# Moving the clamp of the up half from VectorE to GpSimd in a fused adaLN block

## The chip, the cores and the metric

One Trainium2 chip, one core of it. The metric is device microseconds (us) of the whole kernel, lower is better. Engine names are those of the profile: PE (TensorE), with its weight loads as PEld, DVE (VectorE), ACT (ScalarE), POOL (GpSimd), SP (SyncE, which here only issues DMAs).

## The reference, cut to what matters

The input is 8 sequences of 512 tokens of width 128, all in float32. The block is a linear-recurrent "attention" layer followed by a mixture of 8 experts, each behind a modulated layernorm. The change touches the experts alone:

```python
x = x + ga * attn(layernorm(x) * (1 + ca) + sa)     # a scan over the 512 tokens
h = layernorm(x) * (1 + cb) + sb
gate_up = einsum('nd,ejd->nej', h, gate_up_proj) + gate_up_proj_bias   # E = 8, I = 256
gate, up = split(gate_up, 2, axis=-1)
gate = minimum(gate, 7.0)
up = clip(up, -7.0, 7.0)
act = (up + 1.0) * gate * sigmoid(1.702 * gate)
out = einsum('nei,edi->ned', act, down_proj) + down_proj_bias
y = einsum('ned,ne->nd', out, combine)              # softmax over the top 4 of 8 experts
```

## The kernel before

**Tiling and stages.** The tokens are worked through in 16 chunks of 256 (two tiles of 128 rows, 8 sequences x 16 steps each). A chunk passes through seven stages, one iteration of the outer loop apiece: `a` (first layernorm, residual), `g` (gate logits), `e` (softmax of the gates), `s` (the scan of 32 steps), `p` (output projection, second layernorm, router), `m` (the experts) and `o` (write out). In one iteration each engine works on up to seven chunks, each in another stage, so there are 22 iterations. Stage `s` runs in iterations 3 to 18, stage `m` in 5 to 20; iterations 6 to 15 hold all seven stages.

**Order of work.** Every engine has its own instruction stream, written out by hand, and executes it strictly in order; semaphores (`Event`, with `at(c, n)` for the n-th increment of chunk c) tie the streams together. On DVE the scan sets the order: for each step t it issues the products `L758`, then the sums `L766`, and between them the function `between(u, ...)` puts in the other work by slot number u = 3t, 3t+1, 3t+2, thus 96 slots an iteration. Expert k of the stage `m` owns nine slots from u = 22 + 9k on: `clamp_up` (`L831`) at r = 0, and the two halves of `hidden` (`L844`) at r = 3 and 4. Other slots used below: the row sums `L741` at u = 9 to 26 with the reciprocals `L749` at 18 and 28, the row maxima `L734` at odd u from 33 to 67, the output gate `go` (`L896`) at 47 and 49, the statistics of the second layernorm (`L901`) at 56 and 57, and its normalisation `xh2` (`L728`) at 68 and 69.

**One expert.** PE multiplies `h2t` with the up and gate weights (`L997`, in the function `gate_up`, which waits until the activation of expert k-2 is done); ACT evicts the up half to SBUF and adds bias + 1 (`L598`), then puts Silu over the gate half in PSUM (`L604`); `clamp_up` limits the up half in place to 1-7 .. 1+7; `hidden` multiplies both into `act_t`; PE multiplies with the down weights (`L1010`); ACT weighs the result (`L615`); POOL adds it to `yacc` (`L460`, `accumulate`). `up` and `act_t` have two buffers each, by k % 2. `hidden(m, k, 0)` waits for the Silu, for `clamp_ok` and for the down matmul that frees its `act_t` buffer.

**PE's order** within iteration: gate_up(0), gate_up(1), the transposes of the router weights, down(0), bias matmul `L1043`, gate_up(2), the transposes of `yt_tok`, down(1), gate_up(3), the output projection `wo` (`L1031`, on which `go` waits), down(2), gate_up(4), down(3), gate_up(5), down(4), and so on, with the gate logits `L984` in between.

**POOL's order** in an iteration: inverse square root and first h of stage `a`, `finish` of stage `o`, `gate_value(e,0)`, two `norm_gates` (`L407`), `gate_value(e,1)`, accumulate 0, `norm_gates`, `norm_gates`, accumulate 1, `residual`, `sub_max` (`L414`), `new_residual` (`L445`), accumulate 2, `sub_max`, `inv_sqrt` (`L390`, `L393`), accumulate 3, `sub_max`, `second_h` (`L450`, `L452`, it waits for `xh2`), `inv_sqrt`, accumulate 4, `sub_max`, accumulate 5 and 6.

Of the kernel before, what the change touches and what calls it, by code (L numbers as in the profile page):

```python
# [18 lines left out]
ALU = mybir.AluOpType  # L19
# [6 lines left out]
LIMIT = 7.0  # L26
# [21 lines left out]
def adaln_block(nc, x, norm_w, w_v, w_a, w_out, router_w, router_b, gu_w, gu_b, down_w, down_b, cond, w_mod, out):  # L48
# [27 lines left out]
    with ExitStack() as ctx:  # L76
# [87 lines left out]
        up = sb("up", [P, 2, KI * N])  # L164
# [206 lines left out]
        def _(pool):  # L371
# [24 lines left out]
            def gate_value(e, j):  # L396
                pool.wait_ge(zs_ok.sem, zs_ok.at(e, H * (j + 1)))
                v = ex[:, j, :].rearrange("p (r k) -> p r k", k=M1)
                nc.gpsimd.tensor_tensor(v[:, :, 0], v[:, :, 0], vv[:, j, :], ALU.mult).then_inc(rv_ok.sem, 1)

            def norm_gates(e, j, part):
                if part == 0:
                    pool.wait_ge(rz_ok.sem, rz_ok.at(e, j + 1))
                    pool.wait_ge(rv_ok.sem, rv_ok.at(e, j + 1))
                lo, hi = part * HI // 2, (part + 1) * HI // 2
                v = ex[:, j, :].rearrange("p (r k) -> p r k", k=M1)[:, lo:hi, :]
                nc.gpsimd.tensor_tensor(v, v, rz[:, j, lo:hi].unsqueeze(2).broadcast_to([P, HI // 2, M1]),  # L407
                                        ALU.mult).then_inc(norm_ok.sem, 1)
# [19 lines left out]
            def residual(a):  # L428

                if not is_first(a):  # L430
                    for j in range(TILES):
                        pool.wait_ge(res_st[j].sem, res_st[j].at(a, 0))
                pool.wait_ge(h_ok.sem, h_ok.at(a, 1))
                nc.gpsimd.tensor_tensor(res[:, :, :], hh[:, :, :], both(2), ALU.mult).then_inc(gh_ok.sem, 1)
                pool.wait_ge(gh_ok.sem, gh_ok.at(a, 1))
                nc.gpsimd.tensor_tensor(res[:, :, :], res[:, :, :], xg[:, :, :], ALU.add).then_inc(res_ok.sem, 1)
# [17 lines left out]
            def accumulate(m, k):  # L454
# [3 lines left out]
                else:  # L458
                    pool.wait_ge(acc_ok.sem, acc_ok.at(m, k))
                nc.gpsimd.tensor_tensor(yacc[:, :, :], yacc[:, :, :], weighted[:, k % 2, :, :], ALU.add  # L460
                                        ).then_inc(acc_ok.sem, 1)

            def finish(o):
                accumulate(o, E - 1)
                pool.wait_ge(acc_ok.sem, acc_ok.at(o, E))
                nc.gpsimd.tensor_tensor(gy[:, :, :], yacc[:, :, :], both(5), ALU.mult).then_inc(gy_ok.sem, 1)
                if not is_first(o):
                    for j in range(TILES):
                        pool.wait_ge(out_st[j].sem, out_st[j].at(o, 0))
                pool.wait_ge(xm_ld.sem, xm_ld.at(o, 16))  # L470
                pool.wait_ge(gy_ok.sem, gy_ok.at(o, 1))
                nc.gpsimd.tensor_tensor(res_out[:, :, :], gy[:, :, :], xm[:, :, :], ALU.add).then_inc(ro_ok.sem, 1)

            def run(a, g, e, s, p, m, o):
                if a is not None:
                    pool.wait_ge(mv1_ok.sem, mv1_ok.at(a, TILES))
                    inv_sqrt(mv1[:, :, 1], eps_mean, ve1, rs1, ve1_ok, rs1_ok, a)
                    first_h(a)
                if o is not None:
                    finish(o)  # L480
                if e is not None:
                    gate_value(e, 0)
                    norm_gates(e, 0, 0)
                    norm_gates(e, 0, 1)
                    gate_value(e, 1)
                if m is not None:
                    accumulate(m, 0)
                if e is not None:
                    norm_gates(e, 1, 0)
                    norm_gates(e, 1, 1)  # L490
                if m is not None:
                    accumulate(m, 1)
                if a is not None:
                    residual(a)
                if g is not None:
                    sub_max(g, 0, 0)
                if p is not None:
                    new_residual(p)
                if m is not None:
                    accumulate(m, 2)  # L500
                if g is not None:
                    sub_max(g, 0, 1)
                if p is not None:
                    pool.wait_ge(mv2_ok.sem, mv2_ok.at(p, TILES))
                    inv_sqrt(mv2[:, :, 1], eps_mean, ve2, rs2, ve2_ok, rs2_ok, p)
                if m is not None:
                    accumulate(m, 3)
                if g is not None:
                    sub_max(g, 1, 0)
                if p is not None:  # L510
                    second_h(p)
                if a is not None:
                    pool.wait_ge(ms_ok.sem, ms_ok.at(a, TILES))
                    if g is not None:
                        pool.wait_ge(lg_ev.sem, lg_ev.at(g, TILES * KL))
                    inv_sqrt(ms[:, :, 0], eps_sum, me, rms, me_ok, rms_ok, a)
                if m is not None:
                    accumulate(m, 4)
                if g is not None:
                    sub_max(g, 1, 1)  # L520
                if m is not None:
                    accumulate(m, 5)
                    accumulate(m, 6)

            whole(pool, run)
# [141 lines left out]
        def _(dve):  # L667
# [158 lines left out]
                                            rrec[:, :].unsqueeze(2).broadcast_to([P, TILES, E]),  # L826
                                            ALU.mult).then_inc(weigh.sem, 1)

            def clamp_up(m, k):
                dve.wait_ge(up_ok.sem, up_ok.at(m, k + 1))  # L830
                nc.vector.tensor_scalar(up[:, k % 2, :], up[:, k % 2, :], 1.0 + LIMIT, 1.0 - LIMIT,  # L831
                                        ALU.min, ALU.max).then_inc(clamp_ok.sem, 1)

            def hidden(m, k, q):

                if q == 0:
# [15 lines left out]
            def between(u, a, g, e, p, m):  # L852


                if m is not None:
                    if u in (10, 12, 14, 16, 18):
                        combine_weights(m, (u - 10) // 2)
                    if u >= 22 and u < 22 + 9 * E:
                        k, r = (u - 22) // 9, (u - 22) % 9
                        if r == 0:  # L860
                            clamp_up(m, k)
                        if r in (3, 4):
                            hidden(m, k, r - 3)

                if e is not None:
                    if 9 <= u < 17:
                        row_sum(e, 0, u - 9)
                    if u == 18:
                        row_inverse(e, 0)
                    if 19 <= u < 27:  # L870
                        row_sum(e, 1, u - 19)
                    if u == 28:
                        row_inverse(e, 1)

                if g is not None:
                    if 33 <= u < 49 and u % 2:
                        row_max(g, 0, (u - 33) // 2)
                    if 53 <= u < 69 and u % 2:
                        row_max(g, 1, (u - 53) // 2)

                if a is not None:
                    if u in (1, 2):
                        dve.wait_ge(x_in[u - 1].sem, x_in[u - 1].at(a, 16))
                        nc.vector.bn_stats(st1[:, u - 1, :], xg[:, u - 1, :]).then_inc(st1_ok.sem, 1)
                    if u == 4:
                        for j in range(TILES):
                            aggregate(st1, mv1, st1_ok, mv1_ok, a, j)
                    if u == 8:
                        for j in range(TILES):
                            normalise(xh, xg, mv1, rs1, rs1_ok, xh_ok, a, j)  # L890

                if p is not None:
                    if u in (47, 49):
                        j = (u - 47) // 2
                        dve.wait_ge(o_ps.sem, o_ps.at(p, 1))
                        nc.vector.tensor_tensor(go[:, j, :], bank_a(j), mod[:, 2, :], ALU.mult  # L896
                                                ).then_inc(go_ok.sem, 1)
                    if u in (56, 57):
                        j = u - 56
                        dve.wait_ge(xn_ok.sem, xn_ok.at(p, 1))  # L900
                        nc.vector.bn_stats(st2[:, j, :], xn[:, j, :]).then_inc(st2_ok.sem, 1)  # L901
                    if u == 58:
                        for j in range(TILES):
                            aggregate(st2, mv2, st2_ok, mv2_ok, p, j)
                    if u in (68, 69):
                        normalise(xh2, xn, mv2, rs2, rs2_ok, xh2_ok, p, u - 68)
                    if u in (86, 87, 90, 92, 93):
                        router_ranks(p, (86, 87, 90, 92, 93).index(u))
# [196 lines left out]
```

## Time and profile before

| | |
|---|---|
| median of three runs | 946.82 us (946.27 to 947.31) |
| the profiled execution | 945.81 us, of which the span from first to last instruction is 944.1 us |
| mean granted TensorE clock | 0.818 of full speed |
| DVE busy | 836.2 us, 89% of the span |
| PE busy | 641.1 us, 68% |
| ACT busy | 529.3 us, 56% |
| POOL busy | 517.0 us, 55% |
| clamps (`L831`) on DVE | 128, together 79.3 us, and 21.5 us of waiting in front of them |

Busy time leaves out register, semaphore and DMA-issuing instructions. Consecutive instructions of DVE overlap a little: the next one starts about 0.08 us before the recorded end of the one in front, so what an instruction costs its engine is read from start to start. In the middle of the run an iteration repeats every 53.2 us; the one from 481.3 to 534.5 us is the one read in most rows.

### The profile page before, as it was taken

What the parts mean: (1) busy time and instruction counts of PE and PEld (TensorE: products, weight loads), DVE (VectorE), ACT (ScalarE), POOL (GpSimd) and SP (SyncE); (2) the same over time, 40 slices, a digit from 0 to 9 for tenths busy, and PEclk for the clock granted to TensorE, in tenths of its full rate; (3) what the DMA queues carried; (4) which work ended last, traced back from release to release, by engine and by line L of the source; (5) the groups of instructions that cost most, each with busy time, mean ns of one, the idle gap of its engine ahead of it and who ended that gap; (6) DMA issues with size and microseconds to landing.
All of it is one profiled execution on the core that took longest, in us unless ns stands there. A gap on an engine that the chain in (4) does not pass through costs nothing.

```text
span 944.1 us, 11922 instructions
## 1 busy us (share of the span) xinstructions
PE 641.1 (68%) x2762; PEld 477.6 (51%) x2762; DVE 836.2 (89%) x2441; ACT 529.3 (56%) x1203; POOL 517.0 (55%) x539
## 2 busy tenths in 40 slices
PE   5544243585869767675859777676859777677786
PEld 4211022363646556464646555464647556566686
DVE  3455999999999999999999999999999999998753
ACT  3443321475765746475666746475766756364686
POOL 0584655574756565674756565574756464531243
PEclk9875665697977978697977978797978977797998
DMA  7035755554636353555636353545537352552000
GB/s 210 23 82 118 159 104 116 109 112 96 134 70 144 67 111 73 113 111 101 128 70 148 66 114 73 109 108 107 122 70 148 62 133 53 112 112 48 19 15 7
DMA packets 101670, 91.60 MB, mean 97 GB/s; under 512 B 43688, under 2 KB 98272, under 8 KB 99424
## 3 DMA queue, kind: packets, MB, share of 16 engines
q1 hardware_dynamic: 101600, 90.84, 45.4%
q14 instruction: 48, 0.39, 0.2%
q8 instruction: 22, 0.36, 0.2%
HBM read 46.76 MB, written 41.94 MB: 94 GB/s over the span
## 4 chain that ended last, share of the span: by engine, by line
DVE 67%; PE 16%; issue 7%; POOL 4%; SPq 2%; DMA 2%; ACT 2%; DVEq 0%; POOLq 0%; ACTq 0%
DVE prod L758 16%; DVE ps L766 15%; DVE zs L741 8%; DVE act_t L844 7%; DVE up L831 6%; DVE nmax L734 6%; PE ps L997 6%; PE ps L1010 5%; PE ps L984 3%; PE ps L1043 2%; DVE rz L749 2%; DVE xh L728 2%; ACT up L598 1%; POOL rs L393 1%; DMA gu_rows<-_L_ffn_gate_up_proj_dram 1%
## 5 line engine op out<-in xcount | busy, mean ns | idle before, releaser
L997 PE MATMUL ps<-h2t,wgu 128*128 128x256 f32 x1024 | 280.7, 424 | 0.6 <-ACT up L598 0.6
L1010 PE MATMUL ps<-wd,act_t 128*128 128x128 f32 x1024 | 168.6, 316 | 165.6 <-DVE act_t L844 165.6
L1010 PEld LDWEIGHTS ps<-wd,act_t 128*128 128x128 f32 x1024 | 150.5, 221 | 202.3 <-DVE act_t L844 190.0
L997 PEld LDWEIGHTS ps<-h2t,wgu 128*128 128x128 f32 x1024 | 218.4, 219 | 61.4 <-issue 29.8
L766 DVE TENSOR_REDUCE ps<-prod 64x16 f32<-64x272 f32 x512 | 220.1, 430 | 9.9
L758 DVE TENSOR_TENSOR prod<-gates,ps 64x272 f32<-64x272 f32 x512 | 213.9, 418 | 16.4 <-DMA gates<-gate_dram 14.3
L984 PE MATMUL ps<-wl,ht 128*128 128x512 f32 (+1 forms) x320 | 173.9, 649 | 53.1 <-ACT lg L581 43.1
L460 POOL TENSOR_TENSOR yacc<-yacc,weighted 128x256 f32<-128x256 f32 x128 | 94.2, 736 | 144.7 <-ACT weighted L615 144.7
L407 POOL TENSOR_TENSOR ex<-ex,rz 128x1088 f32<-128x1088 f32 x64 | 131.6, 2078 | 14.3 <-DVE rz L749 14.1
L414 POOL TENSOR_TENSOR lg<-lg,nmax 128x1088 f32<-128x1088 f32 x64 | 132.3, 2070 | 3.5 <-DVE nmax L734 3.5
L615 ACT ACTIVATE weighted<-ps,comb 128x128 f32<-128x128 f32 x256 | 79.8, 363 | 82.1 <-PE ps L1010 81.3
L598 ACT ACTIVATE up<-ps,bgu 128x256 f32<-128x256 f32 x256 | 107.5, 473 | 28.6 <-PE ps L997 27.4
L581 ACT ACTIVATE lg<-ps,rms 128x512 f32<-128x512 f32 x128 | 86.2, 687 | 45.5 <-PE ps L984 45.3
L984 PEld LDWEIGHTS ps<-wl,ht 128*128 128x128 f32 x320 | 61.9, 221 | 94.3 <-ACT lg L581 62.2
L604 ACT ACTIVATE ps<-ps,bgu 128x256 f32<-128x256 f32 x256 | 104.5, 450 | 8.7 <-PE ps L997 6.8
L734 DVE TENSOR_REDUCE nmax<-lg 128x16 f32<-128x272 f32 x256 | 104.7, 418 | 0.0
L844 DVE SCALAR_TENSOR_TENSOR act_t<-ps,up 128x256 f32<-128x256 f32 x256 | 97.3, 407 | 7.3 <-ACT ps L604 7.2
L741 DVE TENSOR_REDUCE zs<-ex 128x16 f32<-128x272 f32 x256 | 102.2, 418 | 0.0
L831 DVE TENSOR_SCALAR up<-up 128x512 f32<-128x512 f32 x128 | 79.3, 620 | 21.5 <-ACT up L598 21.5
L390 POOL TENSOR_TENSOR ve<-mv,eps_mean 128x2 f32<-128x2 f32 x32 | 6.3, 197 | 136.2 <-DVE mv L850 136.2
L570 ACT ACTIVATE ex<-lg 128x2176 f32<-128x2176 f32 x32 | 62.9, 2003 | 30.5 <-POOL lg L414 30.5
L640 ACT ACTIVATE yacc<-ps 128x256 f32<-128x256 f32 x16 | 6.1, 384 | 110.3 <-PE ps L1043 110.3
(119 smaller groups left out, 568.3 us busy)
## 6 DMA issues: line engine op xcount, KB each, us to landing
gate_dram<-ex SPq DMA_DIRECT2D x256, 136.0 KB, 3.0
gates<-gate_dram SPq DMA_DIRECT2D x32, 1088.0 KB, 8.3
yt_tok<-y_dram SPq DMA_DIRECT2D x256, 8.0 KB, 5.6
xg<-in_L_attn_x_dram SPq DMA_DIRECT2D x32, 64.0 KB
out_dram<-res SPq DMA_DIRECT2D x32, 64.0 KB
y_dram<-ys SPq DMA_DIRECT2D x32, 64.0 KB, 2.2
r_in<-out_dram SPq DMA_DIRECT2D x32, 64.0 KB
xm<-xn SPq DMA_DIRECT2D x16, 128.0 KB, 3.1
```

Source lines behind the costliest of these rows:

```text
L407: nc.gpsimd.tensor_tensor(v, v, rz[:, j, lo:hi].unsqueeze(2).broadcast_to([P, HI // 2, M1]), ALU.mult).then_inc(norm_ok.sem, 1)
L414: nc.gpsimd.tensor_tensor(v, v, nmax[:, j, lo:hi].unsqueeze(2).broadcast_to([P, HI // 2, M1]), ALU.add).then_inc(sub_ok.sem, 1)
L598: last = nc.scalar.activation(up[:, k % 2, q * N:(q + 1) * N], gu_ps(m, k, 0)[:, q * N:(q + 1) * N], ACT.Identity, bias=bgu[:, k, KI + q:K ...
L734: nc.vector.tensor_reduce(nmax[:, j, h * M:(h + 1) * M], lg[:, j, h * M * M1:(h + 1) * M * M1].rearrange("p (r k) -> p r k", k=M1), AX_X, ...
L741: nc.vector.tensor_reduce(zs[:, j, h * M:(h + 1) * M], ex[:, j, h * M * M1:(h + 1) * M * M1].rearrange("p (r k) -> p r k", k=M1), AX_X, AL ...
L758: nc.vector.tensor_tensor(prod[:, :].rearrange("p (i k) -> p i k", k=M1), gates[:, t, :].rearrange("p (i k) -> p i k", k=M1), state[:, (t ...
L766: nc.vector.tensor_reduce(state[:, t % TS, 1:M1], prod[:, :].rearrange("p (i k) -> p i k", k=M1), AX_X, ALU.add).then_inc(scan.sem, 1)
L831: nc.vector.tensor_scalar(up[:, k % 2, :], up[:, k % 2, :], 1.0 + LIMIT, 1.0 - LIMIT, ALU.min, ALU.max).then_inc(clamp_ok.sem, 1)
L844: nc.vector.scalar_tensor_tensor(out=act_t[:, k % 2, cols], in0=gu_ps(m, k, 1)[:, cols], scalar=SILU_LIMIT, in1=up[:, k % 2, cols], op0=AL ...
L984: nc.tensor.matmul(ps[:, n % 2, 0:w], ht[:, j * P:(j + 1) * P], wl[:, k * LC:k * LC + w], start=True, stop=True).then_inc(lg_ps.sem, 1)
L997: last = nc.tensor.matmul(gu_ps(m, k, which)[:, q * N:(q + 1) * N], wgu[:, k, rows + q * P:rows + (q + 1) * P], h2t[:, m % 2, :], start=Tr ...
L1010: last = nc.tensor.matmul(dn_ps(j), act_t[:, k % 2, q * N + j * P:q * N + (j + 1) * P], wd[:, k, q, :], start=(q == 0), stop=(q == KI - 1))
```

## The change

The function `clamp_up`, with its wait for `up_ok`, the same arithmetic and the same increment of `clamp_ok`, goes from the VectorE block to the GpSimd block. On VectorE the call at r = 0 is gone; on GpSimd eight calls are put between the other work of an iteration. No buffer, wait of another instruction or other order changes.

```diff
+            def clamp_up(m, k):
+                pool.wait_ge(up_ok.sem, up_ok.at(m, k + 1))
+                nc.gpsimd.tensor_scalar(up[:, k % 2, :], up[:, k % 2, :], 1.0 + LIMIT, 1.0 - LIMIT,
+                                        ALU.min, ALU.max).then_inc(clamp_ok.sem, 1)
...
                 if e is not None:
                     gate_value(e, 0)
+                if m is not None:
+                    clamp_up(m, 0)
+                if e is not None:
                     norm_gates(e, 0, 0)
                     norm_gates(e, 0, 1)
+                if m is not None:
+                    clamp_up(m, 1)
+                if e is not None:
                     gate_value(e, 1)
                 if m is not None:
                     accumulate(m, 0)
                 if e is not None:
                     norm_gates(e, 1, 0)
+                if m is not None:
+                    clamp_up(m, 2)
+                if e is not None:
                     norm_gates(e, 1, 1)
                 if m is not None:
                     accumulate(m, 1)
                 if a is not None:
                     residual(a)
+                if m is not None:
+                    clamp_up(m, 3)
                 if g is not None:
                     sub_max(g, 0, 0)
                 if p is not None:
                     new_residual(p)
                 if m is not None:
                     accumulate(m, 2)
+                    clamp_up(m, 4)
                 if g is not None:
                     sub_max(g, 0, 1)
...
                     accumulate(m, 3)
+                    clamp_up(m, 5)
                 if g is not None:
                     sub_max(g, 1, 0)
...
                     accumulate(m, 4)
+                    clamp_up(m, 6)
                 if g is not None:
                     sub_max(g, 1, 1)
                 if m is not None:
                     accumulate(m, 5)
+                    clamp_up(m, 7)
                     accumulate(m, 6)
...
-            def clamp_up(m, k):
-                dve.wait_ge(up_ok.sem, up_ok.at(m, k + 1))
-                nc.vector.tensor_scalar(up[:, k % 2, :], up[:, k % 2, :], 1.0 + LIMIT, 1.0 - LIMIT,
-                                        ALU.min, ALU.max).then_inc(clamp_ok.sem, 1)
...
                         k, r = (u - 22) // 9, (u - 22) % 9
-                        if r == 0:
-                            clamp_up(m, k)
                         if r in (3, 4):
                             hidden(m, k, r - 3)
```

## Rows read from the trace of the kernel before

**Rows 1.** Page, part 1: busy time, share of the span, instructions.

```profile
PE 641.1 (68%) x2762; PEld 477.6 (51%) x2762; DVE 836.2 (89%) x2441; ACT 529.3 (56%) x1203; POOL 517.0 (55%) x539
```

**Rows 2.** Page, part 4: the chain that ended last, by engine.

```profile
DVE 67%; PE 16%; issue 7%; POOL 4%; SPq 2%; DMA 2%; ACT 2%; DVEq 0%; POOLq 0%; ACTq 0%
```

**Rows 3.** One iteration's window: us, then PE, PEld, DVE, ACT, POOL busy, clock, DMA.

```profile
481.30:534.50 53.20, 39.33 (x170) 29.86 (x169) 51.47 (x152) 32.27 (x75) 32.27 (x33) 0.82 0.49 102
```

**Rows 4.** The same window, clamps (L831) alone: DVE busy, clock, DMA.

```profile
481.30:534.50 53.20, 5.46 (x8) 0.82 0.49 102
```

**Rows 5.** All clamps of the run: duration in ns, min/median/max.

```profile
L831 DVE TENSOR_SCALAR up<-up x128: 404/409/1896, 175.8 to 934.8; 128x512 f32<-128x512 f32 x128
```

**Rows 6.** Groups by line and shape on POOL: busy us, mean ns, idle before.

```profile
L414 POOL TENSOR_TENSOR lg<-lg,nmax 128x1088 f32<-128x1088 f32 x64 | 132.3, 2070 | 3.5 <-DVE nmax L734 3.5
...
L460 POOL TENSOR_TENSOR yacc<-yacc,weighted 128x256 f32<-128x256 f32 x128 | 94.2, 736 | 144.7 <-ACT weighted L615 144.7
...
L393 POOL TENSOR_TENSOR rs<-ve,minus_half 128x2 f32<-128x2 f32 x32 | 22.4, 701 | 2.5
...
L390 POOL TENSOR_TENSOR ve<-mv,eps_mean 128x2 f32<-128x2 f32 x32 | 6.3, 197 | 136.2 <-DVE mv L850 136.2
...
L372 POOL MEMSET ident<- 128x128 f32 x1 | 0.2, 205 | 0.3 <-POOLq L1092 0.3
...
L373 POOL MEMSET lower<- 128x64 f32 x1 | 0.2, 153 | 0.0
```

**Rows 7.** Timeline of DVE, that iteration: start us, us, instruction, idle before.

```profile
493.69 0.47 DVE L831 TENSOR_SCALAR up<-up 128x512 f32<-128x512 f32 x1
...
504.77 1.39 DVE L831 TENSOR_SCALAR up<-up 128x512 f32<-128x512 f32 x1 [0.57 <-ACT up L598]
...
507.24 0.40 DVE L844 SCALAR_TENSOR_TENSOR act_t<-ps,up 128x256 f32<-128x256 f32 x1
...
510.15 0.27 DVE L896 TENSOR_TENSOR go<-ps,mod 128x128 f32<-128x128 f32 x1
...
522.16 0.33 DVE L728 TENSOR_SCALAR xh<-xn,mv,rs 128x128 f32<-128x128 f32 x1
...
525.77 0.94 DVE L831 TENSOR_SCALAR up<-up 128x512 f32<-128x512 f32 x1
...
527.44 0.74 DVE L844 SCALAR_TENSOR_TENSOR act_t<-ps,up 128x256 f32<-128x256 f32 x2
```

**Rows 8.** Timeline of PE, the same iteration.

```profile
496.93 2.08 PE L1010 MATMUL ps<-wd,act_t 128*128 128x128 f32 x8 [5.59 <-DVE act_t L844]
...
509.36 0.61 PE L1031 MATMUL ps<-wo,yt 128*128 128x128 f32 x4
...
519.43 1.16 PE L1010 MATMUL ps<-wd,act_t 128*128 128x128 f32 x8 [1.21 <-DVE act_t L844]
```

**Rows 9.** Timeline of POOL, the same iteration.

```profile
501.85 4.03 POOL L407 TENSOR_TENSOR ex<-ex,rz 128x1088 f32<-128x1088 f32 x2
...
518.95 2.04 POOL L414 TENSOR_TENSOR lg<-lg,nmax 128x1088 f32<-128x1088 f32 x1
...
523.17 0.72 POOL L450 TENSOR_TENSOR h<-xh,mod 128x256 f32<-128x256 f32 x1 [2.19 <-DVE xh L728]
...
526.39 2.22 POOL L414 TENSOR_TENSOR lg<-lg,nmax 128x1088 f32<-128x1088 f32 x1
```

**Rows 10.** Timeline of ACT: Silu of expert 2, up half of expert 4.

```profile
505.43 0.81 ACT L604 ACTIVATE ps<-ps,bgu 128x256 f32<-128x256 f32 x2 [0.69 <-PE ps L997]
...
513.79 0.82 ACT L598 ACTIVATE up<-ps,bgu 128x256 f32<-128x256 f32 x2
```

**Rows 11.** The iteration before it: the projection on PE, `go` on DVE.

```profile
455.75 0.61 PE L1031 MATMUL ps<-wo,yt 128*128 128x128 f32 x4
...
457.53 0.28 DVE L896 TENSOR_TENSOR go<-ps,mod 128x128 f32<-128x128 f32 x1
```

**Rows 12.** Timeline of DVE in the last iteration, expert 3.

```profile
925.11 0.76 DVE L844 SCALAR_TENSOR_TENSOR act_t<-ps,up 128x256 f32<-128x256 f32 x2 [0.41 <-ACT ps L604]
```

## The prediction

> **What bounds the kernel now.** I read the busy times first, then the chain, then one iteration in order of time. DVE is busy 89% of the span and no other engine over 68% [rows 1]; 67% of the chain that ended last is DVE [rows 2]. In one full iteration of 53.2 us DVE works 51.47 us while PE works 39.33 and POOL 32.27 [rows 3]. So work taken off DVE can count, but DVE is not alone: PE's timeline has a second chain. From 496.93, when hidden(0) releases down(0), PE works through without a wait until 519.43, where it waits 1.21 us for DVE again [rows 8]. The reader is to see that between those times DVE can run ahead only until it needs something of PE: the Silu of expert 2, and `go`, which needs the projection that PE ends at 509.36 + 0.61 = 509.97 [rows 8], only 0.18 us before `go` starts at 510.15 [rows 7].
>
> **What is removed.** Eight clamps an iteration are busy 5.46 us [rows 4]; with the 0.57 us of waiting in front of the one at 504.77 and less some 0.08 us of overlap each, that is 5.46 + 0.57 - 0.64 = 5.4 us of DVE's 53.2. Five cost 0.33 to 0.38 us from start to start, three cost more. These three are lengthened by POOL: the fastest clamp takes 404 ns, the slowest 1896 [rows 5], and the one at 504.77 ends at 506.16, 0.28 us after POOL's `norm_gates` pair ends at 505.88 [rows 7, 9]. A clamp on DVE stands still until POOL's instruction is over. By expert: 0.38, 0.34, 1.89 (with the wait), 0.95, 0.33, 0.33, 0.86, 0.33.
>
> **What is added.** POOL gets 128 clamps of 128x512; no row shows this operation on it. From the sides: a memset grows from 153 to 205 ns between 64 and 128 columns, 0.81 ns a column, so 512 would take 0.52 us, the lower bound: it reads nothing. An add of two tensors takes 736 ns at 256 columns and 2070 at 1088, 1.6 ns a column and 0.33 us fixed, thus 1.14 us at 512, a bound from above if the second tensor costs more than the second arithmetic step [rows 6]. Below nothing is impossible, as POOL executes it in its stream. I take the fixed part of the add and the column rate of the memset, the nearest for one stream: 0.33 + 512 x 0.81 ns = 0.74 us. An operation can still be dear by its arithmetic: the power takes 701 ns for two columns where the add takes 197 [rows 6]. The GPSIMD Engine Reference of the Trainium skill (4.1, Engine selection) speaks against the move, recommending VectorE for elementwise work on a tile, though one-input operations run roughly at line rate on GpSimd. By its 3.1, 1.03 cycles per element at 1.2 GHz, the 512 columns would take an estimated 0.44 us beside the fixed part, and the sum hardly changes.
>
> **Where the gain goes: a walk through the iteration**, with 0.74 us per clamp. Clamp 0 gone: hidden(0) is 0.38 earlier, and so is PE's chain from down(0). Experts 1 and 2 would free another 0.34 + 1.89, but hidden(2) now waits for its Silu: 505.43 + 0.81 - 0.38 = 505.86, against 507.24 before, 1.3 earlier [rows 7, 10]. Then `go` waits for 509.97 - 0.38 = 509.59; it starts 0.5 us earlier than at 510.15 [rows 7, 8]. So PE's chain takes back 2.6 - 0.5 = 2.1 us. In the iteration before, PE is quicker in this stretch: the projection ends at 455.75 + 0.61 = 456.36 and `go` starts at 457.53, so there 1.5 us would remain [rows 11].
>
> After `go` the offset grows: with clamp 3 to 1.45, clamp 4 to 1.78, clamp 5 to 2.11; normalisation `xh2`, at 522.16 before, is due at 520.05 [rows 7]. On POOL, up 4 is evicted by 513.79 + 0.82 - 0.38 = 514.23 [rows 10], and POOL waits for it with everything behind it. Clamp 4 ends at 515.0, the second `sub_max` 517.1, the inverse root (0.2 + 0.7) 518.05, accumulate 3 518.75, clamp 5 519.5, and the third `sub_max` lies at 519.5 to 521.55 where it lay at 518.95 to 520.99 [rows 6, 9]. Two things are late next.
>
> First, `xh2` (`L728`) is a TENSOR_SCALAR from SBUF to SBUF like the clamp, and now falls into that `sub_max`. If it blocks as the clamps do, it is done at 521.8 only, DVE keeps 0.7 us of its 2.11, and the second tile of `xh2` ends at 522.5. No row has the two together; the clamps are the nearest, so I take the block. Second, clamp 6 stands behind `second_h` (1.5), the inverse root (0.95) and accumulate 4 (0.73): 522.5 + 1.5 + 0.95 + 0.75 + 0.74 = 526.5. Hidden(6), at 527.44 before, would be ready at 527.44 - 0.66 - 0.86 = 525.9 and starts at 526.55, 0.9 earlier [rows 7, 9]. Clamp 7 behind `sub_max` (2.04) and accumulate 5 ends at 530.0, just when hidden(7) is ready. With clamp 7 off DVE the iteration ends 0.9 + 0.33 = 1.2 us earlier; in the quick half of the iterations some 0.4 more, 1.4 on average.
>
> Who waits for the rest of POOL's queue? Nothing soon: the last `sub_max` ends 527.8 against 528.6 before [rows 9], the second `norm_gates` pair slips from 505.9 to 507.2 but its gates are scanned half an iteration later, so SP's stores and loads have room. `new_residual` stands behind clamp 3 and is done by 513.0, before DVE's statistics at 513.8.
>
> **The sum.** Iterations 5 to 15: 11 x 1.4 = 15.4 us. Iteration 16 has no stage `a`, hence a shorter queue before clamp 6: 2.7 us by the same walk. 17 and 18 lack the row maxima and `sub_max`; five or six short clamps of 0.33 count, 2 us each. In 19 and 20 no scan runs: after its clamp DVE waits 0.41 us more for Silu [rows 12], so a POOL clamp 0.33 us longer fits in; nothing. Together 22 us: the profiled execution's 945.81 goes to 924, and as it lay 1.0 under the median of 946.82, I predict 924.5 us, 2.3% less.
>
> **The rivals.**
>
> *`xh2` does not block on POOL (chance 0.25).* Its instructions take 0.33 us at 128 columns against the clamp's 0.41 at 512, which tells nothing of how it reads. The third `sub_max` then costs DVE nothing, `second_h` starts at 521.6 instead of 522.5, clamp 6 is done at 525.5, and each iteration gains 2.2 to 2.6: 11 x 2.4 + 3.6 + 4 = 34, some 912 us. The page SBUF — State Buffer of the Trainium skill (Who interferes with whom) lists tensor_scalar among the VectorE operations that take the port pair shared with GpSimd for the whole instruction, the other side blocking fully; the clamps agree (506.16 after 505.88), of `xh2` no run shows it.
>
> *The POOL clamp is dear (0.15): slower.* The place is the same queue. From up 4 to clamp 7 there are four clamps in a row, so each 0.1 us more on one costs 0.4 us an iteration; the average gain of 1.4 is used up at 0.74 + 1.4/4 = 1.1 us, and with the tail the kernel is no faster from about 1.2 us on. At 1.14 us the iterations give nothing, 16 to 18 about 4 us and 19 and 20 cost 0.3 for some 14 clamps: 946. At 2 us, a power-like price, each iteration loses 4 x 0.86 = 3.4: 985 us or more. The steady column rates speak against it, the unseen arithmetic for it.
>
> *Offloading brings the whole 5.4 us (0.05).* 16 x 5.4 = 86 us less, 860 us; PE's chain [rows 8] speaks against it, unless PE's clock rises in that stretch.
>
> *Nothing changes (0.05).* The handover between engines and POOL's waits eat the gain; a price between 1.1 and 1.2 us does it.
>
> The forecast, with a POOL clamp of 0.52 to 1.0 us, has 0.5.
>
> **The numbers.** The forecast's own range is 914 (0.52 us a clamp: 4 x 0.22 x 11 = 10 less) to 937 (1.0 us: 11 more and a little in the tail). With the second case below it and part of the dear clamp above, 906 to 946 holds eight in ten. The measurement can tell 0.2%, 1.9 us. Faster: 0.5 + 0.25 + 0.05 and a little of the dear case, 0.82. Same 0.05. Slower 0.13.
>
> **What would show it.** The POOL group of the clamp with a mean near 0.74 us. DVE waiting for ACT (Silu) at hidden(2) and for PE at `go` by 0.8 to 1.3 us in every iteration; `L728` over `xn` lengthened from 0.33 to over 1 us in its first tile; DVE waiting for POOL (`clamp_ok`) at hidden(6) by some 0.6 us; an iteration of 51.8 us; DVE's share falling to (836 - 79)/922 = 82%, POOL's rising to (517 + 95)/922 = 66%. I am wrong if the mean of the clamp leaves 0.52 to 1.14, or if the POOL queue is late elsewhere, say at clamp 3 or `new_residual`.

## The result and the profile after

The changed kernel takes 924.22 us (median of 4, 923.26 to 925.54) against 947.07 us (median of 4, 946.27 to 947.42): a ratio of 0.9761, 95% interval 0.9744 to 0.9778, so 2.4% faster. The forecast was 924.5 us. The profiled execution took 925.54 us, its span is 923.8.

The page of the changed kernel, parts 1 and 4, answers to [rows 1, 2]:

```profile
PE 637.9 (69%) x2762; PEld 473.4 (51%) x2762; DVE 785.9 (85%) x2313; ACT 529.3 (57%) x1203; POOL 590.8 (64%) x667
...
DVE 53%; PE 28%; POOL 8%; issue 6%; SPq 2%; DMA 2%; ACT 1%; DVEq 0%; POOLq 0%; ACTq 0%
```

DVE lost 50.3 us of busy time, not the 79.3 us of the clamps; its share of the chain went from 67% to 53%, and PE's from 16% to 28%. Half of the other 29 us is in the next views: the clamps' line on POOL and that of the normalisation `xh2` (`L728` before, `L748` now), in ns min/median/max, and then the group of `xh2`, now and before. Most of the rest, an estimate, is the overlap of 0.08 us between consecutive instructions: 128 x 0.08 = 10 us, counted in full in the clamps' 79.3 us but only once in the busy time of the engine.

```profile
L465 POOL TENSOR_SCALAR up<-up x128: 614/614/617, 175.8 to 914.6; 128x512 f32<-128x512 f32 x128
...
L748 DVE TENSOR_SCALAR xh<-xn,mv,rs x32: 328/332/1556, 156.3 to 883.4; 128x128 f32<-128x128 f32 x32
...
L748 DVE TENSOR_SCALAR xh<-xn,mv,rs 128x128 f32<-128x128 f32 x32 | 25.1, 787 | 0.2 <-POOL rs L393 0.2
...
L728 DVE TENSOR_SCALAR xh<-xn,mv,rs 128x128 f32<-128x128 f32 x32 | 10.5, 332 | 0.0
```

A clamp on POOL takes 0.61 us, every one of the 128. `xh2` grew from 0.33 us a piece to a mean of 0.79, 14.6 us in all. The iteration that answers to [rows 7], on DVE:

```profile
490.11 0.41 DVE L859 SCALAR_TENSOR_TENSOR act_t<-ps,up 128x256 f32<-128x256 f32 x1
...
500.38 0.42 DVE L859 SCALAR_TENSOR_TENSOR act_t<-ps,up 128x256 f32<-128x256 f32 x1 [0.92 <-ACT ps L624]
...
504.11 0.29 DVE L909 TENSOR_TENSOR go<-ps,mod 128x128 f32<-128x128 f32 x1 [0.73 <-PE ps L1044]
...
514.52 1.55 DVE L748 TENSOR_SCALAR xh<-xn,mv,rs 128x128 f32<-128x128 f32 x1
516.34 0.33 DVE L748 TENSOR_SCALAR xh<-xn,mv,rs 128x128 f32<-128x128 f32 x1
...
520.70 0.76 DVE L859 SCALAR_TENSOR_TENSOR act_t<-ps,up 128x256 f32<-128x256 f32 x2 [0.34 <-POOL up L465]
```

PE in the same iteration, down(0) and the projection, to be held against [rows 8]:

```profile
491.24 2.08 PE L1023 MATMUL ps<-wd,act_t 128*128 128x128 f32 x8 [5.00 <-DVE act_t L859]
...
503.46 0.61 PE L1044 MATMUL ps<-wo,yt 128*128 128x128 f32 x4
```

And POOL, to be held against [rows 9]:

```profile
508.80 0.61 POOL L465 TENSOR_SCALAR up<-up 128x512 f32<-128x512 f32 x1 [0.54 <-ACT up L618]
...
513.95 2.04 POOL L414 TENSOR_TENSOR lg<-lg,nmax 128x1088 f32<-128x1088 f32 x1
...
516.75 0.73 POOL L450 TENSOR_TENSOR h<-xh,mod 128x256 f32<-128x256 f32 x1 [0.77 <-DVE xh L748]
...
520.00 0.61 POOL L465 TENSOR_SCALAR up<-up 128x512 f32<-128x512 f32 x1
```

The rows show all three losses of the walk. DVE waits 0.92 us for the Silu of expert 2 and 0.73 us for the projection. `xh2`, due at 514.52 in the middle of the third `sub_max` (513.95 to 515.99), ends at 516.07, 0.08 us after it. `second_h` follows that, clamp 6 stands behind it and ends at 520.61, and hidden(6), at 520.70, has waited 0.34 us for it. DVE's waits over ten full iterations (us, times, longest), first of the changed kernel:

```profile
DVE go L909 <- PE ps L1044: 7.7, 10, 1.1
DVE act_t L859 <- ACT ps L624: 6.6, 8, 1.3
DVE act_t L859 <- POOL up L465: 3.4, 10, 0.3
DVE xh L748 <- POOL rs L393: 3.0, 10, 0.3
DVE rl L804 <- PE ps L1083: 3.0, 5, 0.6
```

and of the kernel before:

```profile
DVE up L831 <- ACT up L598: 4.1, 10, 0.6
DVE xh L728 <- POOL rs L393: 3.0, 10, 0.3
```

The period of an iteration is read from the start of the last step of the router weights, `comb` (`L825` before), to its start one iteration later. Before, the first is at 172.82 and the eleventh at 702.55, a mean of 52.97 us; after, 175.41 and 691.64, 51.62 us. That is 1.35 us less an iteration on average, 13.5 us in ten. From the eleventh to the sixteenth `comb` (702.55 to 913.74 before, 691.64 to 893.44 after) another 9.4 us are gained, 22.9 us together; the stretch behind the last one is 30.3 us before and 30.4 after. In front of the first, where no clamp runs yet, the profiled execution of the changed kernel is 2.6 us later. That need not be the change: in the eleven kernels below the first `comb` starts anywhere between 173.7 and 177.1 us, and the 172.82 of the kernel before is the earliest of all.

### The profile page after: what moved, and what is told of

It is laid out like the page before. It is cut to its first block, busy times and chain, and to the rows that moved or that the text cites. A ratio compares the mean times of both kernels' runs of the same rounds, so it can differ in the third digit from the quotient of the medians.

```text
span 923.8 us, 11922 instructions
## 1 busy us (share of the span) xinstructions
PE 637.9 (69%) x2762; PEld 473.4 (51%) x2762; DVE 785.9 (85%) x2313; ACT 529.3 (57%) x1203; POOL 590.8 (64%) x667
## 4 chain that ended last, share of the span: by engine, by line
DVE 53%; PE 28%; POOL 8%; issue 6%; SPq 2%; DMA 2%; ACT 1%; DVEq 0%; POOLq 0%; ACTq 0%
DVE prod L778 13%; DVE ps L786 12%; PE ps L1010 12%; DVE zs L761 8%; PE ps L1023 8%; DVE act_t L859 5%; DVE nmax L754 4%; PE ps L997 4%; DVE xh L748 3%; POOL lg L414 2%; PE ps L1056 2%; DVE rz L769 2%; POOL rs L393 1%; DMA gu_rows<-_L_ffn_gate_up_proj_dram 1%; SPq L330 1%
## 5 line engine op out<-in xcount | busy, mean ns | idle before, releaser
L1023 PE MATMUL ps<-wd,act_t 128*128 128x128 f32 x1024 | 161.2, 307 | 137.8 <-DVE act_t L859 137.8
L1023 PEld LDWEIGHTS ps<-wd,act_t 128*128 128x128 f32 x1024 | 145.7, 214 | 172.0 <-DVE act_t L859 158.7
L414 POOL TENSOR_TENSOR lg<-lg,nmax 128x1088 f32<-128x1088 f32 x64 | 130.3, 2039 | 7.4 <-DVE nmax L754 3.5
L407 POOL TENSOR_TENSOR ex<-ex,rz 128x1088 f32<-128x1088 f32 x64 | 129.7, 2039 | 6.4 <-DVE rz L769 4.1
L465 POOL TENSOR_SCALAR up<-up 128x512 f32<-128x512 f32 x128 | 78.6, 614 | 33.1 <-ACT up L618 25.4
```

The lines of the kernel that those rows point to most:

```text
L414: nc.gpsimd.tensor_tensor(v, v, nmax[:, j, lo:hi].unsqueeze(2).broadcast_to([P, HI // 2, M1]), ALU.add).then_inc(sub_ok.sem, 1)
L1023: last = nc.tensor.matmul(dn_ps(j), act_t[:, k % 2, q * N + j * P:q * N + (j + 1) * P], wd[:, k, q, :], start=(q == 0), stop=(q == KI - 1))
```

## The experiments

Each was timed in rounds against the kernel before on the same chip; ratios are to it, with 95% intervals. The kernel before took 947.0 to 948.3 us in these rounds, so two rows of different rounds compare to within about 1 us. "Period" is the mean of ten iterations as above.

| run | us | ratio | period |
|---|---|---|---|
| changed kernel | 924.22 | 0.976 (0.974 to 0.978) | 51.62 |
| clamps 1, 2 alone on POOL | 946.14 | 0.998 (0.997 to 0.999) | 52.99 |
| all but 1, 2 on POOL | 922.08 | 0.973 (0.971 to 0.975) | 51.41 |
| doubled for experts 0 to 3 | 939.94 | 0.992 (0.990 to 0.995) | 52.71 |
| doubled for experts 4 to 7 | 951.75 | 1.005 (1.003 to 1.007) | 53.57 |
| `sub_max` late | 909.87 | 0.960 (0.958 to 0.962) | 50.26 |
| before, `sub_max` late | 964.75 | 1.018 (1.015 to 1.022) | 54.41 |
| hidden(0) early | 904.01 | 0.953 (0.949 to 0.957) | 50.01 |
| both edits | 887.29 | 0.937 (0.934 to 0.940) | 48.62 |
| before, hidden(0) early | 949.80 | 1.003 (1.002 to 1.005) | 53.27 |
| clamps 1, 2 on POOL, hidden(0) early | 943.98 | 0.997 (0.996 to 0.998) | 52.94 |
| both edits, hidden(0) six slots early | 884.61 | 0.934 (0.932 to 0.936) | 48.39 |

**Does PE's chain absorb experts 1 and 2?** Two kernels split the clamps between the engines, with a semaphore for each:

```diff
+        ON_POOL = (1, 2)            # the other kernel: (0, 3, 4, 5, 6, 7)
             def clamp_up(m, k):      # POOL
+                if k not in ON_POOL:
+                    return
...
+                        if r == 0 and k in ON_DVE:
+                            clamp_dve(m, k)
```

> Clamps of experts 1 and 2 alone on GpSimd, the other six stay on VectorE. Theory (PE's chain from hidden(0) to the output projection takes back what experts 1 and 2 free): in the iterations with the slower PE stretch go can start only 0.1 us earlier, in the others 1.1 us, so about 0.6 us an iteration: 938 to 942 us. Rival (every clamp taken off VectorE counts): 0.34 + 1.89 us in 16 iterations, 36 us less, 911 us.

> Clamps of experts 1 and 2 back on VectorE, the other six on GpSimd. Theory (PE's chain absorbs these two): at most 0.3 us an iteration above the changed kernel, 924 to 929 us, and VectorE's waits for Silu and for the projection nearly gone. Rival (every clamp counts): 0.34 + 1.9 us in 16 iterations more, 955 us or above.

Measured: 946.14 and 922.08 us. Clamps 1 and 2 on POOL bring 0.2%, and taking them back from the changed kernel costs nothing: the period is 0.2 us shorter, and the time is 2 us under the foreseen 924 to 929. So removing 2.2 us an iteration from DVE between hidden(0) and `go` is worth 0.2% at most; the rival, by which each clamp counts, is out. In the second kernel DVE's wait for `go` is gone but for one of 0.2 us in ten iterations, and that for Silu altogether, as foreseen.

PE's chain alone does not absorb the two clamps, though. In the first kernel `go` starts 0.65 us earlier than before on average over the ten iterations, as foreseen, but its 938 to 942 us were missed: the next clamp, still on DVE, now falls into the first `sub_max`. DVE and POOL there:

```profile
459.79 0.29 DVE L924 TENSOR_TENSOR go<-ps,mod 128x128 f32<-128x128 f32 x1 [0.74 <-PE ps L1059]
460.81 1.65 DVE L856 TENSOR_SCALAR up<-up 128x512 f32<-128x512 f32 x1
...
460.14 2.04 POOL L417 TENSOR_TENSOR lg<-lg,nmax 128x1088 f32<-128x1088 f32 x1
```

The clamp ends at 462.46, 0.28 us after `sub_max` (462.18), and takes 1.65 us instead of 0.41. In the second kernel `go` starts 0.6 us later than in the changed kernel (19.0 against 18.5 us after `comb`, mean of ten), and the period does not grow, as `xh2` loses less there: its group falls from 25.1 to 18.5 us (and a later wait of 0.6 us, told of under the sum below, comes once instead of five times). What PE's chain lets through, the next clash with POOL takes.

**Is the rest of it the queue behind clamp 4?** POOL does one more clamp, of constant weights into a scratch tile, in front of four of the eight:

```diff
+                if k in DOUBLED:     # (4, 5, 6, 7), the other kernel (0, 1, 2, 3)
+                    pool.wait_ge(junk_ok.sem, junk_ok.at(m, DOUBLED.index(k)))
+                    nc.gpsimd.tensor_scalar(junk[:, :], wgu[:, 0, :], 1.0 + LIMIT, 1.0 - LIMIT,
+                                            ALU.min, ALU.max).then_inc(junk_ok.sem, 1)
```

> In front of the clamps of experts 4 to 7 GpSimd does one more clamp of constant weights into a scratch tile (0.61 us each, 0.69 start to start). Theory (these four stand in one queue that sets hidden(6) and hidden(7)): clamp 7 ends 2.8 us later, less what xh2 no longer loses because the third sub_max now starts after it: 1.9 us an iteration more, with the tail 945 to 952 us. Rival (GpSimd has room, 64% busy, only the block of xh2 matters): 924 us or less.

> As the run with a doubled clamp, but for experts 0 to 3. Theory: clamps 0 and 1 lie in gaps of GpSimd; behind clamps 2 and 3 (1.4 us later) clamp 4 has 0.54 us of slack as it waits for the up half, so 0.85 us an iteration is lost: 932 to 936 us, clearly less than with experts 4 to 7 doubled. Rival (GpSimd's total load sets the time): the same loss as with experts 4 to 7.

Measured: 951.75 and 939.94 us, periods 1.95 and 1.09 us over the changed kernel's (foreseen 1.9 and 0.85). The same added work of 4 x 0.61 us costs 27.5 us behind experts 4 to 7 and 15.7 us before; POOL's total load alone would make them equal. With experts 4 to 7 doubled the third `sub_max` starts after `xh2`, which is back at 0.33 us, and the wait has moved to hidden(6):

```profile
470.28 0.33 DVE L755 TENSOR_SCALAR xh<-xn,mv,rs 128x128 f32<-128x128 f32 x1
...
477.83 0.76 DVE L866 SCALAR_TENSOR_TENSOR act_t<-ps,up 128x256 f32<-128x256 f32 x2 [2.92 <-POOL up L472]
```

The early four cost more than foreseen (940 against 932 to 936): `xh2` is blocked longer there, 27.2 us in all against 25.1, and in seven of the ten iterations DVE now waits up to 0.5 us for `new_residual`, which stands behind the doubled clamps.

**What is the block of `xh2` worth?** The two `sub_max` of the second tile go behind clamp 6 and clamp 7, and the same is done, as a control, to the kernel before (there behind accumulate 4 and accumulate 5):

```diff
                     clamp_up(m, 5)
-                if g is not None:
-                    sub_max(g, 1, 0)
...
                     clamp_up(m, 6)
                 if g is not None:
-                    sub_max(g, 1, 1)
+                    sub_max(g, 1, 0)
                 if m is not None:
                     accumulate(m, 5)
                     clamp_up(m, 7)
+                if g is not None:
+                    sub_max(g, 1, 1)
+                if m is not None:
                     accumulate(m, 6)
```

> On GpSimd the third sub_max goes behind clamp 6 and the fourth behind clamp 7; nothing else changes. Theory (the normalisation xh2 on VectorE stands still behind the third sub_max and carries second_h and clamp 6 with it): xh2 falls from 1.55 to 0.33 us and each full iteration gains 1.2 to 1.3 us: 908 to 912 us. Rival (the loss is in the waits for PE and Silu, the block is made up by the wait for clamp 6 anyway): 920 to 924 us.

> Control: the kernel before, clamps on VectorE, with the third and fourth sub_max moved behind accumulate 4 and accumulate 5. Theory (the order helps only where xh2 meets the third sub_max, which it does not before): no gain, and the clamp of expert 7 now falls into the fourth sub_max, up to 1.4 us an iteration: 947 to 962 us. Rival (the new order is better by itself): 932 to 940 us.

Measured: 909.87 us, period 1.36 us less than the changed kernel's, and 964.75 us for the control, 1.8% above the kernel before. The group of `xh2`:

```profile
L749 DVE TENSOR_SCALAR xh<-xn,mv,rs 128x128 f32<-128x128 f32 x32 | 10.9, 344 | 0.2 <-POOL rs L393 0.2
```

It is back at 0.34 us. Without the block the change brings 37 us (947.07 to 909.87) instead of 23, so the block took over a third of that. The new order is no improvement by itself: with the clamps on DVE it is a loss, by more than foreseen (964.75 against 947 to 962), the clamps there growing from a mean of 0.62 to 0.73 us:

```profile
L832 DVE TENSOR_SCALAR up<-up 128x512 f32<-128x512 f32 x128 | 94.0, 734 | 21.8 <-ACT up L599 21.8
```

**What is PE's chain worth?** hidden(0) goes three slots earlier on DVE, alone and with the late `sub_max`; the last kernel has it six slots earlier (`u in (19, 20)`), with the late `sub_max`:

```diff
-                    if u >= 22 and u < 22 + 9 * E:
+                    if u in (22, 23):
+                        hidden(m, 0, u - 22)
+                    if u >= 31 and u < 22 + 9 * E:
```

> The changed kernel with hidden(0) three slots earlier on VectorE (u = 22, 23 instead of 25, 26), nothing else. Theory (PE's chain starts with hidden(0) and ends in the waits of VectorE for Silu of expert 2 and for go, 0.7 to 1.7 us together): the chain starts some 1.8 us earlier, both waits go, 1.3 us an iteration: 906 to 912 us. Rival (GpSimd's queue is the bound behind go, so the time freed is waited away before clamp 6): 920 us or more.

> Both edits together: third and fourth sub_max late on GpSimd, hidden(0) three slots earlier on VectorE. Theory: the two losses are separate and add up, 2.5 us an iteration less than the changed kernel: 893 to 899 us. Rival (one queue behind both): no better than the better of the two alone, 906 to 912 us.

> The best kernel so far (third and fourth sub_max late, hidden(0) early) with hidden(0) six slots early instead of three. Theory (PE's chain is no longer what VectorE waits for, 0.2 us an iteration are left in front of go): 884 to 888 us. Rival (the chain still sets the pace): 878 us or less.

Measured: 904.01, 887.29 and 884.61 us. The first two came out better than foreseen (906 to 912 and 893 to 899), the third in its range. PE's down(0) starts 4.09 us after `comb` instead of 5.80. The chain is worth 1.61 us an iteration, the block 1.36, and both edits together 3.00, where the sum is 2.97: two separate losses. DVE's waits over some four iterations (442 to 645 us), in the kernel with both:

```profile
DVE act_t L860 <- POOL up L465: 1.3, 4, 0.3
DVE xh L749 <- POOL rs L393: 1.2, 4, 0.3
DVE go L912 <- PE ps L1047: 0.7, 1, 0.7
```

and, of the changed kernel, the two that the chain causes:

```profile
DVE act_t L859 <- ACT ps L624: 3.6, 4, 1.2
DVE go L909 <- PE ps L1044: 2.9, 4, 0.7
```

Of these one wait is left. Six slots add 0.23 us an iteration, about what was left in front of `go`; the two last kernels weren't timed in the same rounds and their intervals overlap.

**Controls with hidden(0) early and clamps on DVE.** The kernel before with clamp 0 and hidden(0) three slots earlier, and the same with clamps 1 and 2 on POOL:

```diff
+                    if u == 19:
+                        clamp_up(m, 0)
+                    if u in (22, 23):
+                        hidden(m, 0, u - 22)
```

> Control: the kernel before, all clamps on VectorE, with clamp 0 and hidden(0) three slots earlier. Theory (before, VectorE hardly waits for PE's chain, 0.4 us an iteration, but an earlier accumulate 0 lets the second pair of norm_gates end before clamp 2 comes, which then is not blocked: 0.6 + 1.0 us): 1.5 us an iteration, 928 to 934 us. Rival (nothing in the kernel before hangs on where hidden(0) stands): 944 to 948 us.

> Clamps of experts 1 and 2 on GpSimd as in the first of these runs, now with clamp 0 and hidden(0) three slots earlier. Theory (with PE's chain out of the way the two clamps are worth their plain 0.34 + 0.33 us): 10 us under the kernel before with the same early hidden(0), 918 to 924 us, where the same two clamps brought 2 us without it. Rival (these two are worth nothing wherever hidden(0) stands, for another reason): equal to that control within 3 us.

Measured: 949.80 and 943.98 us. Both missed: 928 to 934 and 918 to 924 were foreseen, the first came out a little above its rival's 944 to 948, and the second lies 5.8 us under the first where 10 were foreseen by the theory and at most 3 by the rival. On DVE clamp 0 now meets the first pair of `norm_gates`, DVE first, then POOL:

```profile
443.08 2.17 DVE L831 TENSOR_SCALAR up<-up 128x512 f32<-128x512 f32 x1
...
442.93 4.21 POOL L407 TENSOR_TENSOR ex<-ex,rz 128x1088 f32<-128x1088 f32 x2 [0.77 <-DVE rz L749]
```

The clamp takes 2.17 us instead of 0.47: it gets its turn between the two instructions of the pair. Clamp 1 takes 0.94 us instead of 0.41; only clamp 2 comes free, as the theory had it. And with that the edit does not do what it was made for. PE's down(0) in this control, and in the same iteration of the kernel before:

```profile
448.02 2.07 PE L1014 MATMUL ps<-wd,act_t 128*128 128x128 f32 x8 [5.59 <-DVE act_t L844]
...
444.31 2.07 PE L1010 MATMUL ps<-wd,act_t 128*128 128x128 f32 x8 [5.59 <-DVE act_t L844]
```

`comb` starts at 441.84 and 438.12, so down(0) comes 6.18 and 6.19 us behind it: three slots are gained and the longer clamp 0 takes them back. The same holds for the second control (6.19). So neither tests what an earlier chain of PE is worth with clamps on DVE; that stays open, and so does why the pair of clamps 1 and 2 is worth 5.8 us here and 2 us in the first of the experiments.

## Why the prediction was right

**The bound.** Right. DVE set the pace before and a chain of PE stood close behind: the early hidden(0) shows that the chain holds the changed kernel back by 1.6 us an iteration, and the split of the clamps that what is freed between hidden(0) and `go` is worth next to nothing, by the chain and the clash behind it together.

**The price on POOL.** Taken as 0.74 us between 0.52 and 1.14; it is 0.614, between the memset's line and the value taken. With one size measured, it stays open whether the fixed part or the column rate was too high. By the walk's own slope, 4 x 0.13 us, this should have made each iteration 0.5 us shorter than forecast.

**The block of `xh2`.** Right in place and kind: 1.55 us for the first tile, 0.33 for the second, in every full iteration; the case that it does not block, at 912 us, is out, and late `sub_max` gives 909.87, near what that case would have been. By the page SBUF — State Buffer of the Trainium skill (Who interferes with whom), a VectorE tensor_scalar can take the port pair that it shares with GpSimd, and whoever issues first then has it for the whole instruction while the other fully blocks. Every clash shown here agrees: the VectorE instruction ends 0.08 to 0.3 us after the GpSimd instruction that it met.

**Clamp 6 and the slope.** Right: hidden(6) waits for clamp 6 by 0.34 us (forecast 0.6 with the dearer clamp), and doubling the clamps of experts 4 to 7 costs 1.95 us an iteration.

**The sum.** 22 us forecast, 22.85 measured between the medians; that they lie so near is in part luck, as errors in the sum cancel. (A small slip as well: 946.82 less 22 is 924.8, not 924.5.) With the true price of the clamp the walk would have given 1.7 us in the slow kind of iteration, that of the rows ahead of the prediction, and 2.1 in the quick kind; 1.35 us came on average. The kinds differ in how long PE takes for gate_up(2), which releases the Silu that DVE waits for, and this follows the clock granted to TensorE in that stretch. Window, us, PE, PEld, DVE, ACT and POOL busy, clock, DMA; first the kernel before, a slow and a quick one, then the changed kernel, an iteration of either kind:

```profile
501.95:505.39 3.44, 3.44 (x11) 2.73 (x10) 2.84 (x8) 1.53 (x3) 3.44 (x2) 0.55 0.22 56
555.18:557.62 2.44, 2.44 (x11) 2.05 (x10) 2.22 (x7) 1.51 (x3) 2.44 (x2) 0.77 0.32 79
...
444.53:448.02 3.49, 3.49 (x11) 2.75 (x10) 3.12 (x9) 1.53 (x3) 2.55 (x2) 0.54 0.32 74
341.00:343.36 2.36, 2.36 (x11) 1.97 (x10) 2.33 (x8) 1.51 (x3) 1.94 (x1) 0.80 0.41 102
```

Before, the two kinds alternate; after, gate_up(2) drifts between 2.4 and 3.6 us over several iterations. Over the ten it takes 2.98 us on average in both kernels, so this moves the gain between iterations and does not change it. Like against like: in the slow kind 53.2 us became 51.7 (the iteration from 433.70), a gain of 1.5. In the quick kind 52.6 became 51.3 (from 330.17), a gain of 1.3 where 2.1 was to be had, and two things were missed there.

First, only the slow kind had a blocked clamp 3 to remove: 1.02 us at 511.15, but 0.41 in the iteration before, at 458.54. Second, DVE waits later, for the router's matmul, which stands on PE behind gate_up(7):

```profile
367.66 0.17 DVE L804 TENSOR_TENSOR rl<-ps,rb 128x16 f32<-128x16 f32 x1 [0.60 <-PE ps L1083]
```

This wait of 0.60 us comes in five of the ten iterations and was in none of my steps. It comes just where the clock falls between the transposes of the second layernorm's result and that matmul. There, with the wait, and in the iteration from 485.44, without it:

```profile
362.75:367.62 4.87, 4.87 (x23) 4.19 (x22) 3.77 (x10) 2.86 (x9) 4.62 (x6) 0.68 0.01 3
518.73:523.02 4.29, 3.61 (x24) 2.96 (x22) 3.74 (x10) 2.87 (x9) 4.12 (x5) 1.00 0.02 6
```

All 15 waits of this kind in the mid-run iterations of these kernels stand at a clock of 0.66 to 0.85 in that stretch, and none at 1.00. In the kernel before the clock is 1.00 there in all ten iterations. With `sub_max` late it is so too and the wait is gone in all ten, so some 0.3 us of the 1.36 of that edit may be the clock's; what decides where in an iteration the clock falls, no run here separates. From the eleventh `comb` to the last 9.4 us were gained, against 1.4 + 6.7 = 8.1 forecast for iterations 15 to 18.

**The signs.** The waits for Silu (up to 1.3 us, in eight of ten iterations) and for `go` (0.7 to 1.1 us, in all), the long `xh2`, the wait for clamp 6 and the iteration of 51.6 us came as named. DVE's share is 85% and not 82%: the 79.3 us of the clamps were taken off whole, without the overlap and without the time that the walk itself gives back to `xh2`.

**The rivals.** A dear clamp: the mechanism is real, its price was not met; at 1.23 us for half of the clamps the kernel falls behind the one before (951.75 us), just past the 1.1 to 1.2 us that were named as the point of no gain. The whole 5.4 us an iteration would have needed the chain and the block out of the way, and even with both edits an iteration is only 3.00 + 1.35 = 4.35 us shorter than before.

## What to carry to other kernels

Work taken off the busiest engine is worth only what the stretch between two of its meetings with another engine's chain lets through: find where the two meet, and count the savings per stretch, not in total. What one meeting lets through can be lost at the next. Before moving an instruction to GpSimd, look for every VectorE instruction that stands still while GpSimd works (here the clamp and `xh2`) and ask which long GpSimd instruction it will fall into once VectorE runs earlier; the order of GpSimd's queue is then as much part of the change as the move. With both mended here (the long `sub_max` behind the last clamps, hidden(0) early) the kernel is 6.3% under the one before, not 2.4%. Late `sub_max` alone makes the kernel before slower; the early hidden(0) did not get earlier there, and both edits together were not tried on it. And look at more than one iteration: the granted clock of TensorE made 1 us of difference in the same matmuls from one to the next.

## What the runs showed of the hardware

A clamp of 128x512 in float32 takes 614 ns on GpSimd, with 3 ns between the fastest and the slowest, and 404 ns on VectorE when undisturbed. So for this operation with one tensor GpSimd needs 1.5 times as long, and less than its own add of two tensors at half the columns (726 ns at 256).

A clamp or an `xh2` on VectorE that meets GpSimd at work waits for the end of that one instruction, not of the queue: `xh2` ends 0.08 us and a clamp 0.28 us after the `sub_max` they fell into, and the clamp at 443.08 slips in between two `norm_gates` issued back to back.

The eight matmuls of one gate_up take 1.89 us where the granted clock is 1.00 (2.4 GHz; at 518.95 in the changed kernel) and 3.62 us where it is 0.50 (1.2 GHz; at 392.30). In the middle of the run the clock falls from one level to the other two or three times in an iteration, and where it falls shifts from one iteration to the next.
